# Gate logits laid out with heads and tokens innermost, the output choice folded into its weights, and one masked multiply moved to a later step

## The reference

```python
gl_v = (x @ Ws).reshape(b, t, h, e)                  # h = 8 heads, e = 5 experts
wv = _topk_mask(gl_v, 2) * jax.nn.sigmoid(gl_v)      # the two largest logits keep their sigmoid
xv = jnp.einsum('btd,edk->btek', x, Wv)
v = jnp.einsum('bthe,btek->bhtk', wv, xv)            # values: a weighted sum over experts
scores = jnp.einsum('bhid,bhjd->bhij', q * scale, k)
attn = jnp.einsum('bhij,bhjd->bihd', jax.nn.softmax(scores, axis=-1), v)
mask_o = _topk_mask((x @ Wd).reshape(b, t, h, e), 2) # the output choice, a mask of 0 and 1
out = jnp.einsum('bthe,bthk,ekd->btd', mask_o, attn, Wo)
```

## Time and profile before

| | |
|---|---|
| median of 3 runs | 2178.54 us (2177.8 to 2180.32) |
| the profiled execution | 2177.41 us, with a span of 2175.7 us |
| PE busy | 1890.0 us, 87% of the span |
| DVE busy | 1634.7 us, 75% |
| ACT busy | 1278.2 us, 59% |
| POOL busy | 1047.6 us, 48% |
| mean granted PE clock | 0.947 |

### The profile page before, as it was taken

One profiled execution on the slowest core, in us unless ns is written; L12 is line 12 of the kernel. 1 busy time (PEld: TensorE's weight loads), 2 busy tenths in 40 slices (PEclk: granted clock), 3 DMA queues, 4 the chain that ended last, 5 costly groups with the idle time before them and its releaser, 6 DMA issues.

```text
span 2175.7 us, 32651 instructions
## 1 busy us (share of the span) xinstructions
PE 1890.0 (87%) x11328; PEld 913.3 (42%) x11328; DVE 1634.7 (75%) x2950; ACT 1278.2 (59%) x2803; POOL 1047.6 (48%) x1124
## 2 busy tenths in 40 slices
PE   1658998999899999989999998999999899998775
PEld 0323544435354443535444353544435354443333
DVE  4548787978778797877879787787978788686561
ACT  0326657575665757566565756657575666657451
POOL 1215365463636556363655636365463646544433
PEclk8879999999999999999999999999999999999977
DMA  3221212020121202012120201212021121200000
GB/s 95 43 34 31 34 41 34 28 36 18 38 31 41 35 28 39 19 36 29 40 35 28 42 26 29 31 35 35 28 42 33 24 29 35 35 6 23 1 10 5
DMA packets 87617, 68.71 MB, mean 32 GB/s; under 512 B 10720, under 2 KB 83104, under 8 KB 87328
## 3 DMA queue, kind: packets, MB, share of 16 engines
q1 hardware_dynamic: 87456, 66.62, 16.3%
HBM read 32.51 MB, written 10.49 MB: 20 GB/s over the span
## 4 chain that ended last, share of the span: by engine, by line
PE 56%; DVE 30%; ACT 7%; issue 3%; DMA 2%; POOL 1%; SPq 0%; POOLq 0%; DVEq 0%; PEldq 0%; ACTq 0%
PE Y L464 8%; DVE nmaxF L849 5%; DVE nmaxA L844 5%; PE S1c L405 4%; PE S1b L405 4%; ACT Pq L684 4%; DVE ztmp L965 4%; PE S2a L429 4%; PE S2b L429 4%; PE M L594 3%; PE S1a L405 3%; PE Y L455 3%; PE M L557 3%; PE M L490 2%; DVE rotated L890 2%
## 5 line engine op out<-in xcount | busy, mean ns | idle before, releaser
L1078 POOL TENSOR_TENSOR Z<-Z,ztmp 128x1280 f32<-128x1280 f32 x112 | 324.5, 2898 | 353.3 <-DVE ztmp L965 351.2
L1045 POOL TENSOR_SCALAR_AFFINE_SELECT PT<-PT 128x256 f32<-128x256 f32 (+1 forms) x640 | 253.5, 406 | 372.8 <-ACT PT L669 368.9
L1069 POOL TENSOR_TENSOR Vf<-Vf,ztmp 128x512 f32<-128x512 f32 x256 | 349.6, 1366 | 146.8 <-DVE ztmp L939 138.3
L464 PE MATMUL Y<-PT,Vf 128*64 128x512 f32 x1024 | 274.8, 617 | 0.0
L669 ACT ACTIVATE PT<-S2a 128x512 f32<-128x512 f32 x320 | 191.3, 598 | 120.0 <-PE S2a L423 119.4
L405 PE MATMUL S1a<-Kf,Qf 64*128 64x512 f32 x352 | 217.5, 700 | 6.6 <-ACT Pq L684 4.6
L939 DVE TENSOR_TENSOR ztmp<-xv,wv_s 128x512 f32<-128x512 f32 x256 | 217.2, 848 | 2.8 <-POOL Z L1078 2.8
L405 PE MATMUL S1c<-Kf,Qf 64*128 64x512 f32 x352 | 207.9, 672 | 12.1 <-ACT Pq L684 10.8
L673 ACT ACTIVATE PT<-S2a 128x512 f32<-128x512 f32 x256 | 153.4, 599 | 89.2 <-PE S2a L429 89.0
L669 ACT ACTIVATE PT<-S2b 128x512 f32<-128x512 f32 x320 | 191.5, 598 | 16.3 <-PE S2b L423 15.7
L405 PE MATMUL S1b<-Kf,Qf 64*128 64x512 f32 x320 | 194.5, 690 | 6.5 <-ACT Pq L684 6.5
(11 more groups left out here) (109 smaller groups left out, 3905.2 us busy)
## 6 DMA issues: line engine op xcount, KB each, us to landing
Qs<-parts SPq DMA_DIRECT2D x96, 128.0 KB
Ks<-parts SPq DMA_DIRECT2D x96, 128.0 KB
tab_s<-in_tab SPq DMA_DIRECT2D x16, 512.0 KB, 4.4
xr<-out_x SPq DMA_DIRECT2D x32, 256.0 KB, 2.9
out_x<-res SPq DMA_DIRECT2D x32, 256.0 KB, 2.2
wa_s<-in_wa SPq DMA_DIRECT2D x16, 320.0 KB, 3.1
xl<-out_x SPq DMA_DIRECT2D x16, 256.0 KB, 2.9
out_x<-in_x SPq DMA_DIRECT2D x8, 256.0 KB, 4.4
```

Of the source, the lines that this page charges most:

```text
L464: last = nc.tensor.matmul(Y[DF * h:DF * h + DF, :], Vf[:, kt, GF * (group - SA) + h, :], PT[:, group % 2, NT * h + kt, :], start=(kt == 0) ...
L1045: last = nc.gpsimd.affine_select(out=v, in_=v, compare_op=ALU.is_ge, fill=0.0, base=0, pattern=pattern, channel_multiplier=-1)
L1069: nc.gpsimd.tensor_tensor(Vf[:, i, :, :], Vf[:, i, :, :], vtmp[:, n % VBUF, :, :], ALU.add).then_inc(v_acc.sem, 1)
L1078: nc.gpsimd.tensor_tensor(Z[:, :, :, :], Z[:, :, :, :], ztmp[:, hh % 2, :, :, :], ALU.add).then_inc(z_acc.sem, 1)
```

## The change

The logits, the counts and the weights get a new layout: experts outermost, then token tiles, then heads, so that the 64 combinations of token tile and head of one expert lie next to each other. The weights Ws and Wd are reordered on the host to match. The comparison table `cmp_` has (rival, expert, head and token) as its order in place of (head and token, expert, rival). The sum over rivals (L904) therefore reads its five addends 640 bytes apart, where they were neighbours.

`f_pick` and the tile `pick` are gone. The weights `wz` are now made in one instruction from `beaten_by` (below 1.5) and the reciprocals, at (6,1), where the product with `pick` was. The masked multiply of the sigmoid moves from (7,4) to (7,9), behind the step at which POOL starts its second sum of the slot.

```diff
-        gate = sb("gate", [P, NT, 2 * HF, E])
+        gate = sb("gate", [P, E, NT, 2 * HF])
-        beaten_by = sb("beaten_by", [P, NT, 2 * HF, E], BF)
-        pick = sb("pick", [P, NT, HF, E])
-        wv_s = sb("wv_s", [P, NT, HF, E])
+        beaten_by = sb("beaten_by", [P, E, NT, 2 * HF], BF)
+        wv_s = sb("wv_s", [P, E, NT, HF])
...
-            "p (g a b) -> p g a b", a=E, b=E)
+            "p (b a g) -> p b a g", a=E, b=E)
...
-                    nc.scalar.activation(gate[:, i, :, :].rearrange("p g e -> p (g e)"), bank(use)[:, 0:NG], ACT.Copy)
+                    nc.scalar.activation(gate[:, :, i, :], bank(use)[:, 0:NG].rearrange("p (e g) -> p e g", e=E), ACT.Copy)
...
-                    last = nc.vector.tensor_tensor(cmp_[:, :, 0:e + 1, e], gl[:, :, e:e + 1].broadcast_to([P, n_gl, e + 1]),
-                                                   gl[:, :, 0:e + 1], ALU.is_gt)
+                    last = nc.vector.tensor_tensor(cmp_[:, e, 0:e + 1, :], gl[:, e:e + 1, :].broadcast_to([P, e + 1, n_gl]),
+                                                   gl[:, 0:e + 1, :], ALU.is_gt)
...
-                        nc.vector.tensor_reduce(by[:, n * half:n * half + n, :], cmp_[:, n * half:n * half + n, :, :],
+                        nc.vector.tensor_reduce(by[:, n * half:n * half + n], beats[:, n * half:n * half + n, :],
                                                 AX.X, ALU.add).then_inc(pick_chain.sem, 1)
...
-                def f_pick():
-
-                    dve.wait_ge(pick_chain.sem, pick_chain.at(j, 6, 2))
-                    nc.vector.tensor_scalar(pick[:, :, :, :].rearrange("p t h e -> p t (h e)"),
-                                            beaten_by[:, :, HF:2 * HF, :].rearrange("p t h e -> p t (h e)"), 1.5, None,
-                                            ALU.is_lt).then_inc(pick_chain.sem, 1)
...
-                        wv_s[:, i, :, e:e + 1].broadcast_to([P, HF, DF]), ALU.mult).then_inc(v_mult.sem, 1)
+                        wv_s[:, e, i, :].unsqueeze(2).broadcast_to([P, HF, DF]), ALU.mult).then_inc(v_mult.sem, 1)
...
-                    nc.vector.tensor_tensor(wz[:, :, :, :], pick[:, :, :, :],
-                                            recF[:, :, :].rearrange("p h t -> p t h").unsqueeze(3).broadcast_to([P, NT, HF, E]),
-                                            ALU.mult).then_inc(mix_chain.sem, 1)
+                    dve.wait_ge(pick_chain.sem, pick_chain.at(j, 3, 2))
+                    nc.vector.scalar_tensor_tensor(
+                        wz[:, :, :, :].rearrange("p e t h -> p e (t h)"), beaten_by[:, :, :, HF:2 * HF], 1.5,
+                        recF[:, :, :].rearrange("p t h -> p (t h)").unsqueeze(1).broadcast_to([P, E, NT * HF]),
+                        ALU.is_lt, ALU.mult).then_inc(mix_chain.sem, 1)
...
-                        if at in ((7, 1), (7, 2), (7, 4)) and f_prep:
-                            f_sigmoid((1, 2, 4).index(b))
-                        if at == (1, 5) and f:
-                            f_pick()
+                        if at in ((7, 1), (7, 2), (7, 9)) and f_prep:
+                            f_sigmoid((1, 2, 9).index(b))
```

More of the change, by code:

```diff
@@ L137, in attention_and_mixture @@
         cmp_ = rotated[:, :, :].rearrange("p a t -> p (a t)").bitcast(BF)[:, 0:NT * 2 * HF * E * E].rearrange(
-            "p (g a b) -> p g a b", a=E, b=E)
-        denF = sb("denF", [P, HF, NT])
-        recF = sb("recF", [P, HF, NT])
-        wz = sb("wz", [P, NT, HF, E])
+            "p (b a g) -> p b a g", a=E, b=E)
+        denF = sb("denF", [P, NT, HF])
+        recF = sb("recF", [P, NT, HF])
+        wz = sb("wz", [P, E, NT, HF])
         Z = sb("Z", [P, NT, E, DF])
@@ L236, in attention_and_mixture @@
         normA_chain = Signal("normA_chain", SA)
-        pick_chain = Signal("pick_chain", 7)
+        pick_chain = Signal("pick_chain", 6)
         mix_chain = Signal("mix_chain", 2)
@@ L685, in exps_f @@
                                          bias=nmaxF[:, GF * g + h, qt:qt + 1],
-                                         accum_out=denF[:, GF * g + h, qt:qt + 1]).then_inc(expF_done.sem, 1)
+                                         accum_out=denF[:, qt, GF * g + h:GF * g + h + 1]).then_inc(expF_done.sem, 1)
                 def rows(group):
@@ L763, in iteration @@
                             act.wait_ge(*drained(j, "F gate3"))
-                            nc.scalar.activation(wv_s[:, :, :, :].rearrange("p t h e -> p t (h e)"),
-                                                 gate[:, :, 0:HF, :].rearrange("p t h e -> p t (h e)"),
+                            nc.scalar.activation(wv_s[:, :, :, :].rearrange("p e t h -> p (e t) h"),
+                                                 gate[:, :, :, 0:HF].rearrange("p e t h -> p (e t) h"),
                                                  ACT.Exp, scale=-1.0).then_inc(sig_e.sem, 1)
@@ L887, in f_compare @@
                         dve.wait_ge(*drained(j, "F gate3"))
-                    gl = gate[:, :, :, :].rearrange("p t g e -> p (t g) e")
+                    gl = gate[:, :, :, :].rearrange("p e t g -> p e (t g)")
                     n_gl = NT * 2 * HF
-                    last = nc.vector.tensor_tensor(cmp_[:, :, 0:e + 1, e], gl[:, :, e:e + 1].broadcast_to([P, n_gl, e + 1]),
-                                                   gl[:, :, 0:e + 1], ALU.is_gt)
+                    last = nc.vector.tensor_tensor(cmp_[:, e, 0:e + 1, :], gl[:, e:e + 1, :].broadcast_to([P, e + 1, n_gl]),
+                                                   gl[:, 0:e + 1, :], ALU.is_gt)
                     if e < E - 1:
-                        last = nc.vector.tensor_tensor(cmp_[:, :, e + 1:E, e],
-                                                       gl[:, :, e:e + 1].broadcast_to([P, n_gl, E - 1 - e]),
-                                                       gl[:, :, e + 1:E], ALU.is_ge)
+                        last = nc.vector.tensor_tensor(cmp_[:, e, e + 1:E, :],
+                                                       gl[:, e:e + 1, :].broadcast_to([P, E - 1 - e, n_gl]),
+                                                       gl[:, e + 1:E, :], ALU.is_ge)
                     else:
@@ L900, in f_count @@
                     dve.wait_ge(pick_chain.sem, pick_chain.at(j, 1, 1))
-                    n = NT * HF
-                    by = beaten_by[:, :, :, :].rearrange("p t g e -> p (t g) e")
+                    n = E * NT * HF
+                    by = beaten_by[:, :, :, :].rearrange("p e t g -> p (e t g)")
+                    beats = cmp_[:, :, :, :].rearrange("p b a g -> p (a g) b")
                     with nc.allow_low_precision(reason="counts of at most 4 are exact in bfloat16"):
-                        nc.vector.tensor_reduce(by[:, n * half:n * half + n, :], cmp_[:, n * half:n * half + n, :, :],
+                        nc.vector.tensor_reduce(by[:, n * half:n * half + n], beats[:, n * half:n * half + n, :],
                                                 AX.X, ALU.add).then_inc(pick_chain.sem, 1)
                 def f_sigmoid(step):
-                    wv2 = wv_s[:, :, :, :].rearrange("p t h e -> p (t h e)")
+                    wv2 = wv_s[:, :, :, :].rearrange("p e t h -> p (e t h)")
                     if step == 0:
@@ L966, in f_mix @@
                                             y[:, :, h:h + 1, :].broadcast_to([P, NT, E, DF]),
-                                            wz[:, :, hh, :].unsqueeze(3).broadcast_to([P, NT, E, DF]),
+                                            wz[:, :, :, hh].rearrange("p e t -> p t e").unsqueeze(3).broadcast_to([P, NT, E, DF]),
                                             ALU.mult).then_inc(z_mult.sem, 1)
@@ L1146 @@
     HE = L0_ffn_Ws.shape[1]
+    gates = np.concatenate([np.asarray(w).reshape(C, HE // E, E) for w in (L0_ffn_Ws, L0_ffn_Wd)], 1)
     arrays = {
@@ L1155 @@
         "wqk": np.concatenate([np.asarray(L0_ffn_Wq), np.asarray(L0_ffn_Wk)], 1),
-        "wgv": np.concatenate([np.asarray(L0_ffn_Ws), np.asarray(L0_ffn_Wd), Wv.transpose(1, 0, 2).reshape(C, E * DH)], 1),
+        "wgv": np.concatenate([gates.transpose(0, 2, 1).reshape(C, 2 * HE), Wv.transpose(1, 0, 2).reshape(C, E * DH)], 1),
         "wo": Wo.reshape(E * DH, C),
```

7 lines of the change are left out of this document (3 added, 4 removed).

## The result

The changed kernel takes 2122.06 us in the median of 5 runs (2114.61 to 2124.22), against 2178.54 us: a ratio of 0.9735, 95% interval 0.9718 to 0.9752. That is 56 us less, where 45 were forecast (2133 us, range 2112 to 2158). The profiled execution is the fastest of the five, 2114.61 us with a span of 2112.9 us, so its trace shows 62.8 us of gain.

A forecast was written before the change was run, and what follows sets the result against it. PE was taken as the bound. Per full iteration 1.26 + 1.1 + 0.73 = 3.09 us, times 14 = 43.3, plus 1.9 for the first: 2177.41 - 45.2 = 2132.2 us profiled, 2133 us as median, range 2112 to 2158.

The forecast's parts named there:

- Output choice removed: At (1,5): PE's 2.16 us wait for S1b goes, POOL's last sum then holds the transposes; gain 1.26 us per iteration.
- The clock behind it: Behind the transposes of Z: the stretch of lower clock disappears; gain 1.1 us per iteration, zero if it stays.
- Comparisons and counts: Slots 6 and 7: comparisons fall to 2.1 us, counts rise to 1.55 us each; DVE's net gain in slot 6 1.85 us.
- The release at (7,3): Behind the product at (7,3): DVE releases the bank earlier, ending PE's wait before L557; gain 0.73 us per iteration.
- Masked multiply moved: From (7,4) to (7,9): it falls from 2.40 to 0.32 us, but the 2.1 us buy PE nothing by themselves.
- First full iteration: DVE holds PE up through slot 7 there, so slot 6's net 1.85 us go straight through: 1.9 us.
- Tail: End of the kernel: it ends on POOL's sums and gains nothing.
- rival 2: The second stretch of lower clock, at 1100 to 1104, may vanish too: 2112 to 2118 us; chance 0.11.
- its own case: The prediction's main case: 2133 us, reaching 2124 to 2142 by the bounds of the counts and first iteration; chance 0.60.
- Rival 1: At the transposes: clock stays low or release stays late; 2148 us, or 2158 if L557 also still waits; chance 0.20.
- Rival 3: At (6,9) and (7,0): slower counts become the bound and delay the release at (7,3); 2191 us; chance 0.04.
- Rival 4: Masked multiply meets POOL again at (7,9) and comparisons keep their rate: about 2170 to 2178 us; chance 0.05.

The follow-up runs named there:

- the fold alone: Kernel before the change, with only the output choice `pick` folded into `wz` (old layout, masked multiply at (7,4)): 2159.31 us, ratio 0.9904.
- The layout alone: Changed kernel with the output choice back at (1,5) and the masked multiply back at (7,4), leaving only the layouts: 2154.54 us, ratio 0.9882.
- the masked multiply back: Changed kernel with the masked multiply returned from (7,9) to (7,4): 2125.43 us, ratio 0.9752.
- the last sum first: Changed kernel with POOL's last sum of Z in slot 1 ahead of its masks of steps 3 and 4: 2133.75 us, ratio 0.9777.
- the counts by additions: Changed kernel with three additions of neighbouring bfloat16 elements in place of the two strided counts: 2118.49 us, ratio 0.9712.
- the rotation later: Changed kernel with the last step of the attention rotation moved on DVE from (3,6) to (3,7): 2101.3 us, ratio 0.9644.
- all three: Changed kernel with the last sum first, the counts by additions and the rotation later together: 2091.08 us, ratio 0.9596.
- the doubled counts: Changed kernel with each count done twice, the first result not used: 2176.92 us, ratio 0.9994.
- without the layouts: Changed kernel with the old layout of logits, counts and weights, output choice still folded and masked multiply still moved: 2150.81 us, ratio 0.9868.

## Why the prediction was right, and where not

By its own steps, per full iteration:

- *Output choice removed, 1.26 us.* Right in mechanism and nearly in size: 1.11 us at the transposes, in the fold alone and in the change alike. The 0.15 us too much are a reading: 1064.71 is where the chain of the earlier trace rows passes to L582, while the first transpose starts at 1064.55 on PE's timeline, 1.10 us behind 1063.45. POOL's last sum is what is late next, for 1.05 us, as forecast.
- *The clock behind it, 1.1 us.* Right at its place, 1.13 us from the transposes to the F scores behind them. It is one of two effects of the clock, though, and the other was a rival only.
- *Comparisons and counts.* By starts the comparisons take 2.3 us (1116.88 to 1117.82 and 1118.49 to 1119.84, where 2.1 were forecast) and the counts 1.53 us each (1.55 forecast). The third of the way for the counts was luck: of an old comparison's three operands only the result hopped, by 10 bytes, while its sources were a repeated element and runs of up to five neighbours. The Trainium skill's rule on hopping reads ("Vector Engine (DVE) Microarchitecture Reference", section 5.2) gave an estimated 1.5 us, and this trace agrees, with 1534 ns for the 800 elements, though these have 2 bytes and the page's words 4.
- *The release at (7,3), 0.73 us.* Mis-sized: 1.20 us. The step counted only the wait that had a row. PE had also been held by DVE at the scores two products earlier, in pieces too short for a row of their own, 0.30 us at S1b and the rest up to L557. The layout alone shows the same 1.20 us.
- *Masked multiply moved, 0.* The step "the 2.1 us buy PE nothing by themselves" holds for slot 7 and fails for slot 1: 0.31 us per iteration there (0.21 when taken back out of the change), 5 us when moved alone. Which of its effects shifts the small copy against POOL's masks was not traced further.
- *First full iteration, 1.9 us.* Wrong: 0.6 us. There PE's waits for DVE shrank in one place (S1b, 2.2 to 0.2 us) and grew in the next (S1c, 2.3 to 2.7, and S1a, 0.9 to 1.4 us).
- *Tail, 0.* Wrong by 4.5 us in the profiled execution. It was taken as bound by POOL's sums alone. From the last comparisons to the end, windows of before and then of now read

```profile
2024.40:2175.70 151.30, 102.24 (x440) 48.82 (x436) 68.83 (x85) 57.75 (x127) 58.36 (x29) 0.77 0.02 6
1966.20:2112.90 146.70, 98.10 (x440) 47.38 (x436) 66.54 (x84) 57.63 (x127) 58.12 (x29) 0.79 0.02 6
```

with the same work and nearly the same waits of PE, among them 17.9 and 17.6 us for POOL's sums. PE's busy time is what shrinks, by 4.1 us, at a higher clock. The step that failed is thus that POOL's sums alone pace the tail; PE's own work between them counts too. With the masked multiply back, the last sum first, the counts by additions, the rotation later and all three the tail took 148.0 to 149.1 us, against 146.7 here and 151.2 before, so part of the 4.5 us belongs to this one execution. What raises the clock there was not tested.

The profiled execution adds up. The 13 middle iterations, ten of 3.8 us and three of 5.4 us, give 53.8 us as read in the trace, the last full one 3.9 us, the start 0.6 us and the tail 4.5 us, 62.8 us together. The forecast of 45 us missed 0.65 us per iteration, the tail, and rival 2 in three iterations. The terms that it had too small outweigh the two too large, so the 2133 us came out 11 us high, and 2122 us lies just under the 2124 to 2142 us of its own case; that the range holds it is owed to the allowance for rival 2. The sum explains the fastest execution. The median is 7.4 us above it, and no trace of an execution at the median says in which iterations. Rival 2 is the one that came true in part: the second stretch of lower clock is absent in some iterations, and the mean clocks of the five executions (0.956 to 0.961) suggest that this is also what spreads them over 9.6 us. Rival 1 (a clock that stays low at the transposes) did not occur, but 1.0 us more of POOL's work brings it back in ten of thirteen iterations. Rival 3 (counts as the bound) is what the doubled counts bring about, at 2.5 us per iteration for 3.1 us of DVE. Rival 4 did not occur: the masked multiply takes 316 ns in its new place.

What stays open is what decides where the clock falls. The same waits, in the same place of the iteration, were followed by no stretch, a single or a double one. It is not chance from one iteration to the next, for the order is regular: in the fold two lengths alternate, without the layouts three (124.8, 123.7 and 123.5 us) come round four times, and with the rotation later every third iteration is the long one. This fits what the prediction says of rival 2, that an iteration of another length may lose the stretch, but no run here tests it by itself.

## What to carry to other kernels

A tiny DVE instruction of a long duration may be waiting inside for POOL, as both did here: see whether an instruction of POOL ends with it, and look for a place where POOL is idle before making the instruction cheaper or folding it away; here moving it was worth as much as removing it. When such a wait goes, follow POOL's own chain to the point that needs it, since that caps the gain. And measure a saving of half a microsecond per iteration on a PE-bound kernel together with the clock: 0.5 us won at one wait came with 12 us lost in the median here (intervals that touch), and the same edit was part of the best version once the rotation stood later. Read every iteration for this, not one: the forms can come in turn.

## What the runs showed of the hardware

Two DVE instructions of 160 elements took 0.23 and 0.32 us where no sum of POOL ran, and 2.65 and 2.40 us where one did, ending within 0.2 us behind it. Comparisons that wrote their bfloat16 results 10 bytes apart ran at 3.2 ns an element by starts, and at 1.4 ns (2.3 us for 1600) along neighbouring elements. A sum over five addends 640 bytes apart took 1534 ns where neighbouring ones took 974 ns. A stretch of lower granted clock cost 1.6 us of iteration time where the waits were otherwise the same. And the length of a wait did not by itself say whether such a stretch follows: with one more microsecond of POOL work, the wait of 2.05 us was followed by one in ten of thirteen iterations and not in the other three.
